# Six of eight expert weight splits done early, stored in DRAM, and loaded back as parts

## The chip, the cores and the metric

The kernel runs on one core of a Trainium2 chip. The metric is the device time of one execution in microseconds (us); smaller is better. The reader needs six names: PE is the matmul engine (TensorE), DVE, ACT and POOL are the vector, scalar and GpSimd engines, SP is the engine that issues most of the transfers, and a DMA queue is where an engine puts its transfers.

## The reference

A block of 16 batches of 128 tokens with 256 features goes through two residual layers. The first is cross-attention with 16 heads beside a gated feed-forward part. The second is a mixture of eight experts, two for each token, and a shared expert for all.

```
x = x + tanh(g_xattn) * (attention(LN(LN(x)), LN(ctx)) @ Wo + (silu(gate) * h) @ Wff2)
xf = LN(x)
shared = silu(xf @ sh_up_w + sh_up_b) @ sh_down_w + sh_down_b
scores = softmax(xf @ gate_w.T); the top 2 of 8, weights made to sum to 1 -> comb
h  = silu(einsum('nd,edh->neh', xf, up_w) + up_b)
ye = einsum('neh,ehd->ned', h, down_w) + down_b
x = x + tanh(g_ffn) * (einsum('ned,ne->nd', ye, comb) + shared)
```

## The kernel before

Every matrix product of f32 values is made of three passes of the PE: each operand is kept as a high part (the value rounded to the PE's format) and a low part (value minus high part), and `matmul3` adds low times high, high times high and high times low. So each weight has to be split once before it is used. The high part is an ACT copy, the low part a POOL subtraction.

The work stands in program order on each engine, written by hand, with semaphores between the engines. There are three stages.

*Attention* is eight passes (`iteration`, groups g = 0 to 7, two batches each) of eight steps s and a tail. In a step PE makes scores and one eighth of the feed-forward part, ACT makes the exponentials (L796) and copies of high parts (L788 for the feed-forward part), POOL scales the probabilities (L614) and makes a low part (L619), and DVE does the rest. In the first four steps POOL also issues one indirect transfer each (`send`, L606) that puts token rows of the pass before into `slot_rows` in DRAM, sorted by expert. SP loads one context tile in each pass and has little else to do from pass 1 to pass 6. In the last pass it writes filler rows to `slot_rows` (L509 to L514).

*The shared stage* follows: `shared_up` and `shared_down` for four blocks of 512 tokens, woven with the routing of the last group. The routing ends with `slot_numbers` on DVE (L1334), behind a wait until the rows of the group before have landed (L1471); it releases POOL's last four sends. `add_shared` (L1387) adds the shared expert's result on DVE.

*The tile loop* goes over 39 tiles of 128 rows. SP fetches a tile (L533, L535) into a ring of four, PE turns it (L1866), ACT and DVE split it (L913, L1504), PE multiplies by the expert's up weights, DVE adds the bias (L1500), ACT applies silu (L924), PE turns the result (L1872) and multiplies by the down weights, ACT scales it (L939), and POOL adds it to the output with an indirect transfer (L723). At tile 0 DVE also computes a table for POOL, `turn_table` (L1430 to L1441), between its work for tile 0 and that for tile 1.

The nine weight sets of this part (`shared` and experts 0 to 7, chunks 0 to 8) come through three staging buffers and one more: SP loads a chunk into a buffer, ACT writes the high part (`expert_hi`, L851, one copy of 128x1024), POOL the low part (`expert_lo`, L600, four subtractions of 128x256), and a chunk is loaded only when the one before it in its buffer is split (L473). Chunks 0 to 2 are loaded in pass 1. Chunk 0 and 1 are split in the last pass, chunk 2 right behind it, and 3 to 8 through the shared stage and into the tile loop, since their places in the big array `weights` hold attention's weights until then. The first four tiles wait for their expert alone, `ring_ready`, e + 2.

```
load_chunk(NCA + 8)                       # SP, L527: waits for the split of chunk 4
sp.wait_ge(dn_freed, USE_DOWN[0] + 2)     # L541, both halves of add_shared(0)
sp.dma_start(tiles_of(out, 0), xs[:, 0:TPS, :]).then_inc(written, 16)
sp.wait_ge(tables_done, 1)
sp.wait_ge(routed, 64 * (NG + 1))         # all sends landed
for t in range(4):
    load_tile(t, t)
```

## Time and profile before

| | |
|---|---|
| median of 3 runs | 549.81 us (549.61 to 549.9) |
| the profiled execution | 549.42 us, with a span of 547.6 us from its first to its last instruction |
| PE busy | 507.1 us, 93% of the span |
| DVE, ACT, POOL busy | 392.9, 329.6, 289.7 us |
| mean granted clock of PE | 0.975 of full speed |

The span is what the trace shows; the execution's own time is 1.8 us more. Times below count from the start of the span. In the pages' busy digits PE is at nine tenths in nearly all slices until about 425 us, then two slices are at 7 and 6; these are the end of the shared stage and the start of the tile loop. Attention lasts until about 404 us and the tile loop starts at about 436 us.

### The profile page before, as it was taken

The numbers are of one execution on the slowest core, as the hardware profiler recorded it, in microseconds if no ns is written. First come the engines' busy times: TensorE is split into PE (matmuls) and PEld (weight loads), VectorE is DVE, ScalarE is ACT, GpSimd is POOL, SyncE is SP. The second block draws the span as 40 slices with busy tenths as digits, with TensorE's granted clock in tenths as the row PEclk, the third lists the DMA queues.
The fourth block names the chain that finished last, engine by engine and source line by source line (L and its number), as shares of the span: only waits on it lengthen the run. The fifth ranks groups of instructions, "written<-read, shape, count | busy, mean of one in ns | idle before, by whom it ended". The sixth has DMA issues, their size and how long they took to land.

```text
span 547.6 us, 14295 instructions
## 1 busy us (share of the span) xinstructions
PE 507.1 (93%) x4081; PEld 489.9 (89%) x4082; DVE 392.9 (72%) x1179; ACT 329.6 (60%) x1074; POOL 289.7 (53%) x331
## 2 busy tenths in 40 slices
PE   7779999999999999999999999999999769998990
PEld 6779999999999999999999999999987759998980
DVE  7697777788787778878777887877687784554540
ACT  3667656656655565675656567565766626675750
POOL 4488535335443533544353354436666955488663
PEclk9999999999999999999999999999999958999996
DMA  5660400000100000010000000002967545588753
GB/s 169 201 219 6 134 13 32 21 2 20 40 0 8 24 28 0 21 37 3 4 27 29 0 20 20 1 12 71 345 183 243 168 136 88 97 131 128 115 79 38
DMA packets 41607, 39.88 MB, mean 73 GB/s; under 512 B 9939, under 2 KB 39588, under 8 KB 41444
## 3 DMA queue, kind: packets, MB, share of 16 engines
q1 hardware_dynamic: 33276, 27.63, 16.6%
q0 software_dynamic: 7968, 11.84, 11.7%
q8 instruction: 14, 0.23, 0.2%
q14 instruction: 19, 0.16, 0.1%
q10 hardware_dynamic: 330, 0.02, 0.0%
HBM read 20.55 MB, written 18.94 MB: 72 GB/s over the span
## 4 chain that ended last, share of the span: by engine, by line
PE 65%; DVE 16%; issue 6%; ACT 5%; DMA 3%; POOL 2%; SPq 1%; DVEq 0%; POOLq 0%; ACTq 0%
PE bank L1524 13%; PE bank L1525 12%; PE bank L1526 12%; PE bank L1605 4%; PE bank L1617 4%; PE bank L1710 4%; PE bank L1700 3%; PE bank L1621 2%; PE bank L1608 2%; DVE norm_probs L996 2%; ACT norm_probs L796 2%; PE bank L1539 2%; PE bank L1715 2%; DMA th<-slot_rows 2%; PE bank L1866 1%
## 5 line engine op out<-in xcount | busy, mean ns | idle before, releaser
L614 POOL TENSOR_TENSOR norm_probs<-norm_probs,rden 128x512 f32<-128x512 f32 x64 | 66.7, 1042 | 113.0 <-DVE rden L1183 112.3
L1524 PE MATMUL bank<-acts,weights 128*128 128x256 f32 x384 | 109.5, 285 | 4.6 <-POOL weights L585 2.2
L1525 PE MATMUL bank<-acts,weights 128*128 128x256 f32 x384 | 108.0, 281 | 0.0
L1526 PE MATMUL bank<-acts,weights 128*128 128x256 f32 x384 | 107.8, 281 | 0.0
L796 ACT ACTIVATE norm_probs<-bank,nmax 128x128 f32<-128x128 f32 x256 | 90.6, 368 | 24.3 <-DVE nmax L1139 24.3
L619 POOL TENSOR_TENSOR acts<-uf,acts 128x256 fp32r<-128x256 f32 x64 | 47.6, 744 | 69.0 <-ACT acts L788 69.0
L723 POOL DMA_INDIRECT out_x<-norm_probs,th x39 | 60.5, 1553 | 31.7 <-DMA out_x<-norm_probs,th 17.8
L1524 PEld LDWEIGHTS bank<-acts,weights 128*128 128x128 f32 x384 | 72.3, 188 | 5.5 <-issue 3.9
L1526 PEld LDWEIGHTS bank<-acts,weights 128*128 128x128 f32 x384 | 72.4, 189 | 0.0
L1525 PEld LDWEIGHTS bank<-acts,weights 128*128 128x128 f32 x384 | 72.3, 188 | 0.0
L788 ACT ACTIVATE acts<-uf 128x256 fp32r<-128x256 f32 x64 | 26.8, 419 | 69.9 <-DVE uf L1208 69.8
L1188 DVE TENSOR_TENSOR acts<-bank,acts 128x512 fp32r<-128x512 f32 x64 | 44.0, 687 | 22.3 <-ACT acts L778 20.2
L796 ACT ACTIVATION_READ_ACCUMULATOR norm_probs<-bank,nmax 128x1 f32 x256 | 52.7, 206 | 0.0
L1710 PE MATMUL bank<-weights,acts 128*128 128x256 f32 x256 | 46.0, 301 | 0.0
L1139 DVE TENSOR_REDUCE nmax<-bank 128x4 f32<-128x512 f32 x64 | 43.7, 682 | 2.2 <-PE bank L1526 1.7
L772 ACT ACTIVATE acts<-bank 128x256 fp32r<-128x256 f32 x64 | 24.4, 382 | 29.7 <-PE bank L1608 29.5
L606 POOL DMA_INDIRECT slot_rows<-spare,routing x36 | 36.4, 1010 | 10.5 <-issue 6.6
L1110 DVE TENSOR_TENSOR acts<-bank,acts 128x256 fp32r<-128x256 f32 x64 | 26.7, 417 | 20.5 <-ACT acts L772 20.2
L1700 PE MATMUL bank<-ident,norm_probs 128*128 128x128 f32 x256 | 38.7, 274 | 2.9 <-POOL norm_probs L614 2.8
L778 ACT ACTIVATE acts<-bank 128x512 fp32r<-128x512 f32 x64 | 38.9, 608 | 3.8 <-PE bank L1700 3.5
L1617 PE MATMUL bank<-weights,acts 128*128 128x256 f32 x256 | 40.4, 280 | 0.0
L1525 PE MATMUL bank<-kz_h,q_t 128*128 128x256 f32 x128 | 36.1, 282 | 0.0
(256 smaller groups left out, 1556.0 us busy)
## 6 DMA issues: line engine op xcount, KB each, us to landing
slot_rows<-tf SPq DMA_DIRECT2D x8, 680.0 KB, 6.7
spare<-slot_rows SPq DMA_DIRECT2D x39, 128.0 KB
ct<-in_ctx SPq DMA_DIRECT2D x8, 256.0 KB, 2.7
xs<-in_x SPq DMA_DIRECT2D x8, 256.0 KB, 5.1
out_x<-xs POOLq DMA_DIRECT2D x3, 512.0 KB, 4.1
stage<-in_L_ffn_up_w SPq DMA_DIRECT2D x5, 256.0 KB, 2.8
stage<-in_L_ffn_down_w SPq DMA_DIRECT2D x5, 256.0 KB, 3.2
xs<-in_L_xattn_Wff SPq DMA_DIRECT2D x4, 256.0 KB
```

What stands on the lines that cost most here:

```text
L614: pool.tensor_tensor(pr[:, s % 2], pr[:, s % 2], rden[:, s % 2, :].unsqueeze(2).broadcast_to((P, 4, P)), ALU.mult).then_inc(probs_ready, 1)
L619: pool.tensor_tensor(uT[1][:, s % 2, :], uf[:, :], uT[0][:, s % 2, :].bitcast(F32), ALU.subtract).then_inc(u_ready, 1)
L723: pool.indirect_dma_start(out_rows, bass.IndirectOffsetOnAxis(ap=meta[:, t, 0:1].bitcast(I32), axis=0), ys[:, at:at + D], None, compute_op ...
L796: done = act.activation(pr[:, s % 2, h, :], sc_ps[s % 2][:, h * P:(h + 1) * P], ACT.Exp, bias=nmax[:, s % 2, h:h + 1], accum_out=den[:, s ...
L1139: dve.tensor_reduce(nmax[:, s % 2, :], halves(sc_ps[s % 2], 4), AX.X, ALU.max, negate=True).then_inc(nmax_done, 1)
L1188: dve.tensor_tensor(pT[1][:, :], t_ps[:, :], pT[0][:, :].bitcast(F32), ALU.subtract).then_inc(pT_ready, 1)
L1524: pe.matmul(ps, wts[1], mov[0], start=first, stop=False, skip_group_check=True)
L1525: pe.matmul(ps, wts[0], mov[0], start=False, stop=False, skip_group_check=True)
L1526: return pe.matmul(ps, wts[0], mov[1], start=False, stop=last, skip_group_check=True)
L1617: pe.matmul(at, oT[0][:, m, :], w[:, 2 * (s // 2) + m, :], start=False, stop=False, skip_group_check=True)
L1700: done = pe.transpose(t_ps[:, h * P:(h + 1) * P], pr[:, (s - 1) % 2, h, :], ident[:, :])
L1710: pe.matmul(out_ps[:, b * D:(b + 1) * D], uT[0][:, (s - 1) % 2, b * P:(b + 1) * P], w[:, s - 1, :], start=s == 1 and b == 0 and n == 0, st ...
```

## The change

The splits of experts 2 to 7 move into passes 1 to 6, one expert a pass. SP loads the expert's weights as they are into the first staging buffer. In steps 2, 4, 5 and 7 of the pass ACT copies a quarter as high part into the second staging buffer and POOL subtracts, in place in the first. Then SP stores both parts into a new DRAM array, `parked`, in the order in which `weights` keeps them. Behind attention SP loads them straight to their places, one transfer of 1 MB for each expert: 2 to 4 behind the last feed-forward product of attention (`mix_filled`), 5 and 6 behind `ff2_done`, 7 behind `wo_done`. Chunks 1 and 2 (experts 0 and 1) are loaded between pass 6 and the filler rows. `ring_ready` now ends at 3, and PE's first tile waits for it and for all six loads (`weights_in`).

```diff
-NPOS = NE + 1
+NPOS = 3
+PARK_FROM = 2
+PARK_STEPS = (2, 4, 5, 7)
@@ SP
-            for c in range(3):
+            load_chunk(NCA)
+            split(sp, 8)
+            split(sp, 9)
+            for g in range(1, NG - 1):
+                if g > 1:
+                    sp.wait_ge(park_stored, 32 * (g - 1))
+                e = PARK_FROM + g - 1
+                for m, w in enumerate((up_w[e], down_w[e])):
+                    sp.dma_start(park_src[:, KT * m:KT * m + KT, :], w.rearrange("(k p) n -> p k n", p=P)
+                                 ).then_inc(stage_full[0], 16)
+                if g + 2 < NG:
+                    load_ctx(g + 2)
+                sp.wait_ge(park_lo, 4 * g)
+                for i, part in enumerate(park_parts):
+                    sp.dma_start(parked[e - PARK_FROM, :, i::2, :],
+                                 part.bitcast(F32).rearrange("p (m k) n -> p m (k n)", m=2)).then_inc(park_stored, 16)
+            sp.wait_ge(park_stored, 32 * (NG - 2))
+            for c in (1, 2):
                 load_chunk(NCA + c)
-            for g in range(3, NG):
-                load_ctx(g)
...
-            for c in range(3, 6):
-                load_chunk(NCA + c)
-            sp.wait_ge(pT_filled, NG * NU)
-            load_chunk(NCA + 6)
-            load_chunk(NCA + 7)
+            sp.wait_ge(mix_filled, mix_index(f"FF{NU - 1}", NG - 1, False, True) + 1)
+            for e in range(PARK_FROM, 5):
+                load_parked(e)
+            sp.wait_ge(ff2_done, NG * NU)
+            load_parked(5)
+            load_parked(6)
             sp.wait_ge(wo_done, NG * NU)
...
-            load_chunk(NCA + 8)
+            load_parked(7)
@@ POOL, in a pass
+                    if s in PARK_STEPS and not first and not last:
+
+                        k = PARK_STEPS.index(s)
+                        pool.wait_ge(park_hi, g * 4 + (k - 3))
+                        pool.tensor_tensor(park_parts[1][:, k], park_src[:, k], park_parts[0][:, k].bitcast(F32),
+                                           ALU.subtract).then_inc(park_lo, 1)
@@ POOL, behind the last pass
-            expert_lo(3)
...
-            expert_lo(4)
-            expert_lo(5)
-            store_tiles(1)
-            expert_lo(6)
-            store_tiles(2)
-            expert_lo(7)
-            store_tiles(3)
-            expert_lo(8)
+            for j in range(1, TPS):
+                store_tiles(j)
@@ ACT, in a pass, behind the tanh of step s
+                    if s in PARK_STEPS and not first and not last:
+
+                        k = PARK_STEPS.index(s)
+                        act.wait_ge(stage_full[0], g * 32 + stage_value(8))
+                        act.activation(park_parts[0][:, k], park_src[:, k], ACT.Copy).then_inc(park_hi, 1)
@@ ACT: expert_hi(3) to expert_hi(8) are gone
@@ PE, first tile
-                    if loop is None and t < 4:
-                        pe.wait_ge(ring_ready, e + 2)
-                    elif loop is None and t == 4:
-                        split(pe, NCA + NE)
+                    if loop is None and t == 0:
+                        pe.wait_ge(ring_ready, NPOS)
+                        pe.wait_ge(weights_in, 16 * (NE - PARK_FROM))
```

On SP, from the end of the filler rows to the first fetch of a tile, this is what stood there before. The `stage`, `xs` and `norm_probs` rows are the chunks to be split.

```order
L514 DMA slot_rows<-ct 128x16 x7
L475 DMA stage<-in_L_ffn_up_w 128x2x256
L475 DMA stage<-in_L_ffn_down_w 128x2x256
...
L475 DMA norm_probs<-in_L_ffn_up_w 128x2x256
L475 DMA norm_probs<-in_L_ffn_down_w 128x2x256
L475 DMA stage<-in_L_ffn_up_w 128x2x256
L475 DMA stage<-in_L_ffn_down_w 128x2x256
L522 DMA acts<-bias_copy 128x2048
L525 DMA acts<-bias_rows 1x2048 x2
...
L542 DMA out_x<-xs 128x4x256
L531 TENSOR_LOAD tf
```

And this stands there now, in the same place (line numbers are those of the changed kernel).

```order
L539 DMA slot_rows<-ct 128x16 x7
L543 DMA weights<-parked 128x2048 x5
L554 DMA acts<-bias_copy 128x2048
L557 DMA acts<-bias_rows 1x2048 x2
L543 DMA weights<-parked 128x2048
L574 DMA out_x<-xs 128x4x256
L563 TENSOR_LOAD tf
```

Twelve transfers of 256 KB that waited for splits have become six of 1 MB that wait for attention's last products alone, and the last of them no longer waits for POOL.

On POOL, from its last sends to its first scatter of the tile loop, this stood before (with the semaphores that each row waits for).

```order
L606 DMA slot_rows<-spare,routing 18816x272 [waits slots_done]
L606 DMA slot_rows<-spare,routing 18816x272 x3
L600 TENSOR_TENSOR weights<-stage,weights 128x256 [waits ring_hi_done]
L600 TENSOR_TENSOR weights<-stage,weights 128x256 x3
L600 TENSOR_TENSOR weights<-xs,weights 128x256 [waits ring_hi_done]
L600 TENSOR_TENSOR weights<-xs,weights 128x256 x3
L695 DMA out_x<-xs 128x4x256 [waits dn_freed]
L600 TENSOR_TENSOR weights<-norm_probs,weights 128x256 [waits ring_hi_done]
L600 TENSOR_TENSOR weights<-norm_probs,weights 128x256 x3
L695 DMA out_x<-xs 128x4x256 [waits dn_freed]
```

Now the same stretch is this.

```order
L638 DMA slot_rows<-spare,routing 18816x272 [waits slots_done]
L638 DMA slot_rows<-spare,routing 18816x272 x3
L732 DMA out_x<-xs 128x4x256 [waits dn_freed] x3
L754 DMA out_x<-norm_probs,th 2560x256 [waits y_added1,y_added0,y_added2,y_copied,y_added3,stored,turns_done,written]
```

The subtractions of chunks 4 to 8, 20 of them, no longer stand between the last send and the first scatter; chunk 3's four stood ahead of the last sends and are gone too.

In a pass of attention POOL has this now in steps 4 and 5. The rows on `stage` are new.

```order
L646 TENSOR_TENSOR norm_probs<-norm_probs,rden 128x512
L651 TENSOR_TENSOR acts<-uf,acts 128x256
L670 REGISTER_ALU
L671 TENSOR_TENSOR stage<-stage 128x256
L645 REGISTER_ALU
L646 TENSOR_TENSOR norm_probs<-norm_probs,rden 128x512
L651 TENSOR_TENSOR acts<-uf,acts 128x256
L662 REGISTER_ALU
L663 TENSOR_TENSOR spare<-spare,routing 128x2x8
L670 REGISTER_ALU
L671 TENSOR_TENSOR stage<-stage 128x256
```

So a part operation stands behind the low part of its step and ahead of the next scaling of probabilities. On PE and DVE the instructions are the same in number and order; only what they wait for differs, at PE's first tile and at the first row of `turn_table`.

## Rows read from the trace of the kernel before

**Rows 1.** The page, its first line.

```profile
span 547.6 us, 14295 instructions
```

**Rows 2.** Stretch, length, busy PE, PEld, DVE, ACT, POOL, PE clock, DMA share, GB/s.

```profile
180.00:232.00 52.00, 51.52 (x435) 50.85 (x434) 41.06 (x134) 32.66 (x120) 23.28 (x27) 1.00 0.06 19
...
440.00:450.00 10.00, 6.21 (x27) 5.22 (x27) 9.09 (x18) 2.08 (x6) 7.09 (x10) 0.50 0.53 160
```

**Rows 3.** The same columns in stretches of 2 us.

```profile
394.00:396.00 2.00, 2.00 (x19) 2.00 (x18) 1.35 (x10) 1.72 (x9) 2.00 (x4) 1.00 1.09 357
...
420.00:422.00 2.00, 2.00 (x15) 1.86 (x15) 1.72 (x12) 0.00 (x0) 0.00 (x0) 1.00 1.03 374
...
438.00:440.00 2.00, 0.95 (x3) 0.56 (x4) 1.88 (x4) 0.38 (x1) 0.00 (x0) 0.54 0.28 68
...
454.00:456.00 2.00, 2.00 (x14) 2.00 (x13) 1.01 (x3) 1.33 (x4) 1.35 (x1) 0.69 0.12 17
```

**Rows 4.** SP in order of time: start, us, engine, line, what.

```profile
402.86 0.43 SPq L475 DMA_DIRECT2D stage<-in_L_ffn_up_w  x1
...
430.88 0.40 SPq L475 DMA_DIRECT2D stage<-in_L_ffn_up_w  x1
...
431.84 0.46 SPq L542 DMA_DIRECT2D out_x<-xs  x1
433.35 0.36 SPq L533 DMA_DIRECT2D spare<-slot_rows  x1
```

**Rows 5.** PE in order of time, with idle time before and releaser.

```profile
436.99 0.41 PE L1866 MATMUL bank<-ident,spare 128*128 128x128 f32 x2 [1.27 <-DMA th<-slot_rows]
...
449.96 0.69 PE L1872 MATMUL bank<-ident,ct 128*128 128x128 f32 x2 [3.29 <-ACT ct L924]
```

**Rows 6.** DVE in order of time, the same columns.

```profile
421.69 0.17 DVE L1334 CAST routing<-routing 128x4 int32<-128x4 f32 x1
...
423.50 0.15 DVE L1403 SCALAR_TENSOR_TENSOR routing<-routing 1x8 f32<-1x8 f32 x1
423.69 0.16 DVE L1405 TENSOR_SCALAR ct<-routing 1x8 f32<-1x8 f32 x1
...
427.65 1.59 DVE L1387 SCALAR_TENSOR_TENSOR xs<-bank,gates,xs 128x512 f32<-128x512 f32 x2
...
437.86 0.42 DVE L1504 TENSOR_TENSOR kz_l<-bank,kz_h 128x256 fp32r<-128x256 f32 x1 [2.95 <-ACT kz_h L913]
...
443.08 0.71 DVE L1431 SCALAR_TENSOR_TENSOR xs<-xs,routing 1x8 f32<-1x8 f32 x1
...
447.28 0.45 DVE L1436 TENSOR_TENSOR xs<-tf,routing 1x294 f32<-1x294 f32 x1
...
449.04 0.42 DVE L1500 TENSOR_TENSOR uf<-bank,acts 128x256 f32<-128x256 f32 x1
```

**Rows 7.** POOL in order of time, behind attention.

```profile
414.14 1.22 POOL L606 DMA_INDIRECT slot_rows<-spare,routing  x1 [0.30 <-issue]
...
426.15 0.96 POOL L606 DMA_INDIRECT slot_rows<-spare,routing  x1 [0.31 <-issue]
...
444.44 2.78 POOL L600 TENSOR_TENSOR weights<-stage,weights 128x256 fp32r<-128x256 f32 x4
```

**Rows 8.** ACT, then POOL, then DVE in one pass.

```profile
194.25 0.42 ACT L788 ACTIVATE acts<-uf 128x256 fp32r<-128x256 f32 x1 [0.69 <-DVE uf L1208]
...
197.25 1.04 POOL L614 TENSOR_TENSOR norm_probs<-norm_probs,rden 128x512 f32<-128x512 f32 x1 [1.75 <-DVE rden L1183]
...
212.30 1.30 POOL L591 TENSOR_TENSOR acts<-tf,acts 128x512 fp32r<-128x512 f32 x1 [0.58 <-ACT acts L742]
...
195.66 0.73 DVE L996 TENSOR_SCALAR norm_probs<-ct,mean,ry 128x256 f32<-128x256 f32 x2
...
206.08 2.06 DVE L996 TENSOR_SCALAR norm_probs<-xs,mean,ry 128x256 f32 x2
```

**Rows 9.** Who waited for whom on PE, 100 to 355 us: total, times, longest.

```profile
PE bank L1621 <- DVE acts L1110: 2.5, 6, 0.5
```

More of the change, by code:

```diff
@@ L264, in program @@
         bias_rows = nc.dram_tensor("bias_rows", (2, 2 * NE + 1, D), F32).ap()
+        parked = nc.dram_tensor("parked", (NE - PARK_FROM, P, 4, KT * HID), F32).ap()
         bias_copy = nc.dram_tensor("bias_copy", (NE, HID), F32).ap()
@@ L283, in program @@
         ring_ready = sem("ring_ready")
+        park_hi = sem("park_hi")
+        park_lo = sem("park_lo")
+        park_stored = sem("park_stored")
+        weights_in = sem("weights_in")
         ident_done = sem("ident_done")
@@ L377, in buffer @@
                 return (stage[:, i, :] if i < 2 else spare[:, 0:1024] if i == 2 else slow_stage), i
-            i = (0, 1, 3, 0, 1, 3, 2, 0, 1)[n - NCA]
-            return (stage[:, i, :] if i < 2 else pr.rearrange("p s h n -> p (s h n)") if i == 2
-                    else slow_stage), i
+            i = (3, 0, 1)[n - NCA]
+            return (stage[:, i, :] if i < 2 else slow_stage), i
+        park_src = stage[:, 0, :].rearrange("p (k n) -> p k n", k=4)
+        park_parts = [stage[:, 1 - i, :].bitcast(F32R).rearrange("p (k n) -> p k n", k=4) for i in range(2)]
         def tile_loop(eng, step):
@@ L435, in stage_value @@
         def stage_value(n):
-            return 16 * sum(len(chunk_loads(m)) for m in range(n + 1) if buffer(m)[1] == buffer(n)[1])
+            parks = 32 * (NG - 2) if n >= NCA and buffer(n)[1] == 0 else 0
+            return 16 * sum(len(chunk_loads(m)) for m in range(n + 1) if buffer(m)[1] == buffer(n)[1]) + parks
         def landed(eng, n):
@@ L514, in _, with load_parked @@
                 sp.dma_start(pads[:, k, D:ROW], pad_pairs[k % 3].rearrange("p e k -> p (e k)")).then_inc(pads_stored, 16)
-            for c in range(3, 6):
-                load_chunk(NCA + c)
-            sp.wait_ge(pT_filled, NG * NU)
-            load_chunk(NCA + 6)
-            load_chunk(NCA + 7)
+            def load_parked(e):
+                sp.dma_start(experts[:, e * 2048:(e + 1) * 2048].bitcast(F32),
+                             parked[e - PARK_FROM].rearrange("p m n -> p (m n)")).then_inc(weights_in, 16)
+            sp.wait_ge(mix_filled, mix_index(f"FF{NU - 1}", NG - 1, False, True) + 1)
[4 more added lines that the diff above has]
+            load_parked(6)
             sp.wait_ge(wo_done, NG * NU)
@@ L564, in _ @@
             pool.dma_start(dbrow[0:1, :], sh_down_b.rearrange("(a n) -> a n", a=1)).then_inc(dbrow_in, 16)
-            pool.dma_start(dbrow[1:NPOS, :], down_b).then_inc(dbrow_in, 16)
+            pool.dma_start(dbrow[1:NE + 1, :], down_b).then_inc(dbrow_in, 16)
             pool.memset(ones.bitcast(F32), 1.0)
@@ L892, in _ @@
             hidden_hi(0)
-            expert_hi(3)
-            expert_hi(4)
             act.wait_ge(dn_filled, USE_X1T + 1)
@@ L931, in tile_step @@
                             act.wait_ge(y_added[n % 4], 16 * (n // 4))
-                        elif n == RING // 2 - 1:
-                            act.wait_ge(ring_ready, NPOS)
                     else:
@@ L1427, in turn_table @@
             def turn_table():
-                dve.wait_ge(ring_ready, NPOS - 3)
+                dve.wait_ge(ring_ready, NPOS)
                 link(dve.tensor_scalar(floor_0, ntiles, -float(P), 2.0 * P, ALU.mult, ALU.add))
```

6 lines of the change are left out of this document (removed).

## The prediction

> **What bounds the kernel now.** I read first the page and then the table of stretches. The profiled execution took 549.42 us, of which the span is 547.6 [rows 1]. In a stretch of attention PE is busy for 51.52 of 52 us, at full clock, while POOL is busy for 23.28 and ACT for 32.66 [rows 2]. From 100 to 355 us only one wait of PE has a length worth listing, 2.5 us in six pieces [rows 9]. So attention is bound by PE, and what the other engines do there is free as long as it comes in time. Between 440 and 450 us PE is busy for 6.21 of 10 us and its clock is at 0.50 of full speed, that is, at the lower of its two levels, 1.2 GHz [rows 2]. This stretch, where the shared stage gives way to the tile loop, is the only one that the change can shorten.
>
> The timelines of the engines say what PE waits for there. It ends the shared stage at 435.72 and waits 1.27 us for the first tile, whose transfers SP issued only at 433.35, behind the store of the first output block at 431.84, behind a chunk that had waited for POOL until 430.88 [rows 4, 5]. The store's own condition, both halves of `add_shared(0)`, had been met at 429.24 (427.65 + 1.59 [rows 6]). Then PE waits once more, 3.29 us before 449.96, for silu of tile 1 [rows 5]. ACT could not give that, since DVE added tile 1's bias only at 449.04 [rows 6]. Before it DVE worked on `turn_table`: six instructions on single rows of 7 or 8 elements, from 443.08 to 447.28, 4.20 us, or 0.70 us each. The same kind of instruction takes one step of 0.19 us at 423.50 [rows 6], when POOL is idle. POOL was subtracting meanwhile; its last four, of chunk 8, start at 444.44 and take 2.78 us [rows 7], and the fast pace of DVE returns as they end.
>
> **The change part by part.** *The first tile comes earlier.* SP no longer waits for POOL. It issues the store at 429.3, right behind 429.24, and the first tile's transfers 1.51 us later (433.35 - 431.84 [rows 4]), at 430.8 instead of 433.35. The tile took 3.6 us from there until PE used it (436.99 - 433.35), so it is there at 434.4, before PE has ended the shared stage. PE then turns it at 435.7 and not at 436.99: the idle 1.27 us are gone. (POOL at rest may also let DVE end its part of the shared stage some tenths earlier; I count nothing for it.) ACT's copy and DVE's subtraction of tile 0 (437.86 [rows 6]), `add_shared(2)`, `add_shared(3)` and the bias of tile 0 follow on each other and move with it: 1.27 us.
>
> *`turn_table` is not slowed.* Its six small instructions take six steps of 0.19 to 0.20 us instead of 4.20: 1.2, a gain of 3.0. Its longer ones came behind POOL's last subtraction already.
>
> The Trainium skill gives a reason for the pace (GPSIMD Engine Reference, Specifications): GpSimd's access to SBUF is shared with the vector engine, in contention with those of its instructions that have two inputs in SBUF or run in a two-port mode. The rows agree in so far as the slow steps end with POOL's work. The same rule speaks against the change in the passes, where POOL gets 24 more subtractions; that is the third rival.
>
> Both terms stand on one chain, DVE to the bias of tile 1, then ACT, then PE: 1.27 + 3.0 = 4.27 us. PE's restart moves from 449.96 to 445.7.
>
> *The clock.* In the trace it is at half from the stretch 438 to 440 (mean 0.54) until the stretch 454 to 456 (0.69, so it rose at 455.2) [rows 3]; PE had been without a gap since 449.96. At half speed these 5.2 us did the work of 2.6. After the change PE still idles in pieces: between 435.7 and 445.7 it has five tiles to turn (0.4 us each as at 436.99 [rows 5]), one silu result and three products of six matmuls, by my estimate 4 to 5 us of work in 10. I take it that the clock falls and comes back about as long after the restart as before: no term, with a rival at 2.6 us.
>
> *The passes.* ACT gets four copies of 128x256 a pass. An instruction of this size is 0.42 us, and the copy stands behind tanh, where ACT then idles for 0.69 us in the tightest step, step 4 [rows 8]. POOL gets four subtractions, 0.70 us each (2.78 for four [rows 7]). In step 4 it idles 1.75 us before the scaling [rows 8], and the part fits. In step 7 it idles 0.58 us before the low part of the next x [rows 8], so that one comes some 0.15 us later; it is wanted only behind the keys and values. SP's transfers are off the others' way: 0.5 MB in and 1 MB out in a pass whose DMA share is 0.06 [rows 2]. ACT waits for the weights in step 2. The store follows step 7 of the pass before; 1.57 MB at 357 GB/s [rows 3] is 4.4 us, and with twice the 3.6 us from issue to use of a tile 11.6. Step 2 comes about a third of a pass behind step 7, and eight passes end at about 404 us, so that is some 16 us. From both sides: nothing at the least, since PE has no wait to lose; at the most what stands under the third rival. I take nothing.
>
> *The loads behind attention.* From 402.86 [rows 4] SP issues six transfers of 1.05 MB and `up_bias` with 1.05 MB: 7.3 MB, twice as much as before. The trace moves 357 GB/s when saturated with stores, and 374 where `up_bias` alone, with rows of 8 KB as these have, goes through [rows 3]. At 357 this is 20.6 us: all is in at 423.5, 7 us before the first tile is fetched on the same queue and 13 before PE needs the weights. It costs nothing by itself. But POOL's four sends of the group before (the last at 414.14 [rows 7]) go through the same engines, and `slot_numbers` (421.69 [rows 6]) waits for them. They have 6.3 us from the end of issue (415.36) to need. A tile's transfer takes 3.6 us on a lightly used queue, which leaves 2.7 us for the crowd.
>
> *Removed from ACT*: six copies of 128x1024, where ACT waited anyway. No term.
>
> **The sum.** 549.42 - 4.27 = 545.15 for the profiled execution. The median of the runs is 0.39 us above it, so 545.5 for the median.
>
> **The rivals.** *The clock stays up* (18 in 100). If PE's pieces of work between 435.7 and 445.7 keep it up, the half-speed work behind the restart is saved too: 545.5 - 2.6 = 542.9. For it: 4 to 5 us of work in 10, against 0.95 in the two microseconds where it fell [rows 3]. Against it: a gap of 2 to 3 us before the restart stays. The Trainium skill says (TensorE: Matmul & The Clock Gate, the HAM clock gate) that a lack of activity throttles the clock to 1.2 GHz and that steady activity releases it; the trace shows both turns, and not where between the two patterns the boundary lies.
>
> *Only the table gains* (12 in 100). The tile's fetch stays as late, behind the stores of output blocks or the last loads on SP's queue: 3.0 us instead of 4.27, 546.8.
>
> *The sends starve* (16 in 100). If a saturated queue of 8 KB rows lets POOL's sends through only when it is empty, at 423.5, and they then take 0.5 us, `slot_numbers` comes at 424.2 and everything behind it 2.5 us later: 545.5 + 2.5 = 548.0. The Trainium skill (DMA: Bandwidth & Descriptors, Queues, rings and completion order) has the engines go round the queues packet by packet, which would let them through; no run here has shown it for rows of this size. This rival ends slower than before only if the loads run at under 7.3 MB / (425.5 - 402.9) = 323 GB/s, since then the delay is over 4.27 us.
>
> *The passes pay* (9 in 100), the one that ends on the other side. DVE's pair of scalings (L996) takes 0.73 us alone and 2.06 us when POOL works through it [rows 8]: 1.33 us more under about two of POOL's instructions, or 0.7 for each. In step 4 a part falls on such a pair (195.66). If PE had no slack behind two of the four parts of a pass, 2 x 0.74 x 6 = 8.9 us would be added: 554.4. It cancels the gain from 0.71 us a pass on (4.27 / 6) and is measurably slower from 0.90. Against it: PE waits for DVE 0.4 us a pass now [rows 9], and in the pair's step POOL and ACT both idle before their next pieces of work [rows 8].
>
> **How the numbers follow.** Forecast 45 in 100, 545.5, its own range 544.3 to 546.7. A measurement of this kernel can tell about 0.2%, 1.1 us. Faster by more: the forecast, the first two rivals and three quarters of the third, 45 + 18 + 12 + 12 = 87, less 3 for what I have not seen: 84. Within: 6. Slower: 10. The range that leaves 2 in 10 out goes from 542.0, below the first rival, to 548.4, above the third.
>
> **What would show it right or wrong.** In the new trace the stretch 100 to 355 has the same PE busy share, and attention still ends at about 404 us; SP's store comes at 429.3 and the first tile at 430.8; the six small rows of `turn_table` take 0.2 us each; PE's first L1872 (now in a new line) stands at about 445.7; the weights are in by 424. It is wrong if ACT's park copies wait for their transfer (then each pass is longer), if the DVE row of `slot_numbers` stands later than 421.7, or if the tile loop from the restart to the end is longer than its 97.7 us now (547.6 - 449.96), for instance because POOL's scatters, which run at the pace of the tiles, were the limit all along.

## The result and the profile after

Over four runs each the changed kernel takes 544.34 us (542.77 to 545.37) against 549.74 us (549.61 to 549.9) for the kernel before; the ratio is 0.9899, with a 95% interval of 0.9875 to 0.9923. Two more measurements, made with the experiments on other occasions, gave 0.9898 (0.9875 to 0.9922) and 0.9907 (0.9887 to 0.9927). The change makes the kernel 1% faster, some 5.4 us. The chips differ in level (one has the kernel before at 546.2 us), so below the times of kernels are compared within a group or as ratios. Of traces from different chips only the lengths of single stretches are compared.

The profiled execution of the changed kernel took 544.31 us, 5.11 less than the one of before, and the span is 5.1 us shorter [rows 1].

The windows, with the columns of [rows 2], show an unchanged pass and a fuller stretch at 440 to 450 us:

```profile
span 542.5 us, 14349 instructions
...
180.00:232.00 52.00, 51.52 (x435) 50.84 (x435) 41.93 (x130) 33.70 (x123) 26.26 (x30) 1.00 0.14 49
440.00:450.00 10.00, 8.14 (x54) 7.75 (x55) 7.13 (x23) 4.69 (x13) 2.33 (x3) 0.83 0.52 159
```

PE is busy for the same 51.52 us of 52, while POOL has 3.0 us and ACT 1.0 us more to do. In the later stretch PE is busy for 8.14 us in place of 6.21. The list of PE's waits from 100 to 355 us is the same to the tenth as in [rows 9]:

```profile
PE bank L1646 <- DVE acts L1135: 2.5, 6, 0.5
```

SP in order of time shows the first loads behind attention, the store of the first output block and the first fetches of tiles ([rows 4]):

```profile
402.89 2.56 SPq L543 DMA_DIRECT2D weights<-parked  x5
...
430.37 0.41 SPq L574 DMA_DIRECT2D out_x<-xs  x1
431.82 0.36 SPq L565 DMA_DIRECT2D spare<-slot_rows  x1
```

PE in order of time: the turns of tiles 0 and 1, and the restart ([rows 5]):

```profile
436.27 0.38 PE L1890 MATMUL bank<-ident,spare 128*128 128x128 f32 x2
437.47 0.44 PE L1890 MATMUL bank<-ident,spare 128*128 128x128 f32 x2 [0.82 <-DMA th<-slot_rows]
...
445.60 0.44 PE L1896 MATMUL bank<-ident,ct 128*128 128x128 f32 x2 [0.62 <-ACT ct L951]
```

DVE in order of time: `slot_numbers`, the first half of `add_shared(0)`, tile 0 with its bias, the short rows of `turn_table`, and the bias of tile 1 ([rows 6]):

```profile
422.81 0.17 DVE L1359 CAST routing<-routing 128x4 int32<-128x4 f32 x1
...
428.75 1.60 DVE L1412 SCALAR_TENSOR_TENSOR xs<-bank,gates,xs 128x512 f32<-128x512 f32 x2
...
437.11 0.42 DVE L1529 TENSOR_TENSOR kz_l<-bank,kz_h 128x256 fp32r<-128x256 f32 x1 [3.11 <-ACT kz_h L940]
...
441.22 0.42 DVE L1525 TENSOR_TENSOR u<-bank,acts 128x256 f32<-128x256 f32 x1 [0.34 <-issue]
...
442.35 0.15 DVE L1458 TENSOR_TENSOR xs<-xs 1x8 f32<-1x8 f32 x1
442.53 0.15 DVE L1459 TENSOR_TENSOR tf<-tf,xs 1x7 f32<-1x7 f32 x1
...
444.68 0.42 DVE L1525 TENSOR_TENSOR uf<-bank,acts 128x256 f32<-128x256 f32 x1
```

The rows of `turn_table` take 0.15 us each. In the kernel before the five behind the first took 0.71, 0.75, 1.38, 0.64 and 0.65 us; this is the longest:

```profile
444.50 1.38 DVE L1433 TENSOR_TENSOR xs<-xs 1x8 f32<-1x8 f32 x1
```

From the bias of tile 0 to that of tile 1 it is 3.46 us now; in the kernel before it was 6.89 us (442.15 to 449.04). PE goes from the shared stage into tile 0 without a wait.

Last the granted clock, the column in front of the last two, in windows of 2 us ([rows 3]):

```profile
402.00:404.00 2.00, 1.42 (x10) 1.42 (x11) 1.93 (x12) 1.10 (x3) 1.21 (x2) 0.83 0.27 30
404.00:406.00 2.00, 2.00 (x11) 2.00 (x11) 0.60 (x1) 0.00 (x0) 0.00 (x0) 0.50 0.82 303
...
440.00:442.00 2.00, 0.76 (x3) 0.76 (x4) 1.56 (x5) 0.52 (x2) 0.89 (x2) 0.72 0.68 236
442.00:444.00 2.00, 2.00 (x12) 2.00 (x11) 1.76 (x9) 0.70 (x3) 0.00 (x0) 0.50 1.00 332
444.00:446.00 2.00, 1.38 (x10) 1.03 (x9) 1.84 (x6) 0.85 (x3) 0.00 (x0) 0.93 0.45 104
```

Before, one fall lasted from 438 to 455 us. Now the clock is at half from 440.9 to 444.3 us (worked out from the means, as are all such times below), and before that from 403.3 to 406.8 us, at the end of attention, where the kernel before had none.

**Where the time went.** Each line is how much earlier (-) or later (+) a landmark stands in the new trace, and what was added since the line above. The last four are ACT's scaling of the results of a tile (L939 before, L964 after) and the end of the span.

```
landmark                                  before   after    diff   added here
PE ends the shared stage                  435.72   436.27  +0.55   clock fall at 403.3, less what DVE gained
PE turns tile 0                           436.99   436.27  -0.72   -1.27  no wait for the tile
DVE adds the bias of tile 0               442.15   441.22  -0.93   -0.21
DVE adds the bias of tile 1               449.04   444.68  -4.36   -3.43  turn_table
PE restarts with the silu of tile 1       449.96   445.60  -4.36    0
ACT scales tile 1                         455.63   449.16  -6.47   -2.11  full clock behind the restart
ACT scales tile 20                        495.97   491.50  -4.47   +2.00  in the tile loop
ACT scales tile 38                        534.49   529.30  -5.19   -0.72  in the tile loop
end of the span                           547.6    542.5   -5.1    +0.1
```

The first line is two things. Behind the fall of the clock `add_shared(0)` starts 1.10 us later (427.65 and 428.75 us). But DVE's next two operations on 128x512 took 2.25 us beside POOL's subtractions before (the first line below) and take 1.37 now; the second line is from e8_after_again, where they stand together. So `add_shared(1)` starts only 0.38 us later (431.33 and 431.71), and from `add_shared(0)` to PE's end of the stage it is 7.52 us now (428.75 to 436.27) and was 8.07 (427.65 to 435.72): 1.10 - 0.55 = 0.55.

```profile
429.16 2.25 DVE L1377 TENSOR_TENSOR q_t<-norm_probs,q_t 128x512 fp32r<-128x512 f32 x2
429.23 1.37 DVE L1402 TENSOR_TENSOR q_t<-norm_probs,q_t 128x512 fp32r<-128x512 f32 x2
```

### The profile page after: what moved, and what is told of

The parts are those of the page before. It is cut to its first block, busy times and chain, and to the rows that moved or that the text cites. A ratio compares the mean times of both kernels' runs of the same rounds, so it can differ in the third digit from the quotient of the medians.

```text
span 542.5 us, 14349 instructions
## 1 busy us (share of the span) xinstructions
PE 505.0 (93%) x4081; PEld 489.4 (90%) x4082; DVE 391.6 (72%) x1179; ACT 330.9 (61%) x1092; POOL 289.2 (53%) x331
## 4 chain that ended last, share of the span: by engine, by line
PE 66%; DVE 16%; issue 7%; ACT 5%; POOL 2%; DMA 2%; SPq 1%; DVEq 0%; POOLq 0%; ACTq 0%
PE bank L1549 13%; PE bank L1550 12%; PE bank L1551 12%; PE bank L1630 4%; PE bank L1735 4%; PE bank L1642 4%; PE bank L1725 3%; PE bank L1633 2%; PE bank L1646 2%; DVE norm_probs L1021 2%; ACT norm_probs L827 2%; PE bank L1564 2%; PE bank L1740 2%; DVE nmax L1164 1%; PE bank L1896 1%
```

## The experiments

Each group ran on one chip. In the first are e1, e2, e4 and e8, with the kernel before at 546.19 us; in the second e3, e5, e6 and e7, with it at 549.57 us; in the third e9 to e12, with it at 549.82 us. The second has no run of the changed kernel, so there the ratios to the kernel before are compared (0.9899, 0.9898 and 0.9907 for the changed kernel). What each was expected to do stands under it as it was written before the run.

**e8_after_again, e11_after_again: the changed kernel itself.**

> The changed kernel unchanged, once more, for how far its executions lie apart. Its first four lay between 542.8 and 545.4 us, and the profiled one showed a fall of the granted clock at 403.5 us for 3.4 us that the kernel before did not have there. Theory A (where the clock falls differs from execution to execution, and with it up to about 2 us): the median lies within 543.5 to 545 us, the spread is again over 1 us, and a profiled execution with another mean clock has its falls elsewhere. Rival B (the fall at 403.5 us belongs to the change): it stands there again in this profile, with the same length.

> The changed kernel once more, as the mark for the other kernels of this group on the same chip. It should lie at 0.990 of the kernel before, as in both measurements so far (0.9899 and 0.9898), within their intervals.

540.75 us (539.8 to 542.18), ratio 0.9898, and 544.67 us (543.19 to 546.09), ratio 0.9907. The first lies under the 543.5 to 545 us expected, on a chip where the kernel before is some 3.5 us faster too; the ratio is the same. The spread is 2.4 and 2.9 us. The falls of the clock in three profiled executions of one and the same kernel, each worked out from windows of 2 us, up to 455 us:

```
first profile                          403.3-406.8   440.9-444.3
e8_after_again    16.8-20.2, 30.4-33.8               440.0-443.4
e11_after_again   16.9-20.3, 30.6-34.0 429.9-433.4   443.6-450.4
```

So the fall at 403.3 us is not in every execution of the changed kernel. In e8_after_again, without it, it is 24.64 us from PE's wait at the end of attention to `add_shared(0)` (403.08 to 427.72), against 24.66 before (402.99 to 427.65), and SP's store and first fetch stand where the prediction had them:

```profile
429.34 0.41 SPq L574 DMA_DIRECT2D out_x<-xs  x1
430.79 0.36 SPq L565 DMA_DIRECT2D spare<-slot_rows  x1
```

In e11_after_again the same stretch is 25.35 us (403.27 to 428.62), with no fall of the clock in it. Here DVE waits for the sends, which it does in neither trace without the loads (before, e10_before_table_early):

```profile
422.68 0.17 DVE L1359 CAST routing<-routing 128x4 int32<-128x4 f32 x1 [0.82 <-DMA slot_rows<-spare,routing]
```

The last of these sends starts at 414.42 us, so it took about 8.3 us to land; the DVE row needs it 7.5 us after its start (421.69 - 414.14 before, 421.79 - 414.25 in e8_after_again). The same wait, of 0.3 to 0.6 us, stands in seven of the other nine traces with the loads. So the loads cost that path between nothing and 0.8 us.

All three profiles show a fall in the gap behind 440 us, and it lasts 3.4 us in two and 6.8 us in the third. The lengths of the stretches from PE's first turn of a tile on are these:

```
stretch                                  before   first   e8      e11
PE's turn of tile 0 to bias of tile 0      5.16    4.95    4.93    4.91
bias of tile 0 to bias of tile 1           6.89    3.46    3.45    3.44
bias of tile 1 to ACT's scaling of it      6.59    4.48    4.45    5.76
scaling of tile 1 to that of tile 20      40.34   42.34   40.56   40.35
scaling of tile 20 to that of tile 38     38.52   37.80   37.70   38.41
```

The shorter table (second line) comes back in all three. What the clock gives behind the restart is 2.1 us in two and 0.8 us in the third. The 2.00 us lost in the tile loop of the first profile are in neither of the others.

**e1_pool_busy: GpSimd subtracts again.**

```diff
-            for j in range(1, TPS):
-                store_tiles(j)
+            filled = [0]
+            def fill(n):
+                for _ in range(n):
+                    if filled[0]:
+                        pool.wait_ge(fill_done, filled[0])
+                    for k in range(4):
+                        done = pool.tensor_tensor(stage[:, 0, 256 * k:256 * k + 256], stage[:, 1, 256 * k:256 * k + 256],
+                                                  stage[:, 1, 256 * (3 - k):256 * (3 - k) + 256], ALU.subtract)
+                    done.then_inc(fill_done, 1)
+                    filled[0] += 1
+            fill(1)
+            store_tiles(1)
+            fill(2)
+            store_tiles(2)
+            fill(1)
+            store_tiles(3)
+            fill(1)
```

> The changed kernel with one addition: after its last sends GpSimd subtracts again, 20 dummy subtractions of 128x256 in groups of four, laid around the three stores of output tiles, into a buffer that nobody reads. They should keep GpSimd busy from about 428 to 447 us as in the kernel before, with nothing waiting for their result. Theory A (the small VectorE operations of `turn_table` are slowed while GpSimd subtracts): the small rows, 0.15 to 0.16 us in the changed kernel at 442.35 to 444.55, go back to about 0.70 us as in [rows 6], the table ends 3.0 to 3.4 us later and the time rises by 2.5 to 3.5 us, to 547 to 548 us. Rival B (the rows became short for a reason that has nothing to do with GpSimd, for example the order of the transfers around them): the rows stay under 0.2 us and the time stays within 1 us of 544.3 us.

543.83 us against 540.75 us for the changed kernel in the same group: 3.1 us slower, ratio 0.9952 (0.9936 to 0.9968). POOL and DVE in order of time:

```profile
440.87 2.80 POOL L743 TENSOR_TENSOR stage<-stage 128x256 f32<-128x256 f32 x4
443.63 0.77 POOL L733 DMA_DIRECT2D out_x<-xs  x1
444.42 3.25 POOL L743 TENSOR_TENSOR stage<-stage 128x256 f32<-128x256 f32 x4
```

```profile
441.72 0.61 DVE L1474 TENSOR_SCALAR xs<-routing 1x8 f32<-1x8 f32 x1
...
443.11 0.58 DVE L1477 TENSOR_TENSOR xs<-xs 1x8 f32<-1x8 f32 x1
443.73 0.15 DVE L1478 TENSOR_TENSOR tf<-tf,xs 1x7 f32<-1x7 f32 x1
...
444.55 0.95 DVE L1480 TENSOR_TENSOR xs<-tf,routing 1x294 f32<-1x294 f32 x1
```

Four of the six short rows, at 441.72, 442.36, 443.11 and 443.92 us, take 0.58 to 0.64 us. The other two, at 442.93 and 443.73, take 0.15, and one with 294 elements takes 0.95 instead of 0.45. Which row is long cannot be read off POOL's row beside it: 443.73 and 443.92 both start while POOL issues the store. The issue too can lengthen a row: in e4_table_early, where POOL subtracts nothing, the table's first row takes 0.48 us (434.96 to 435.44) under the issue of a store (434.65 to 435.48). A row that reduces one input is not longer, though it lies under the subtractions that start at 444.42:

```profile
446.43 0.45 DVE L1484 TENSOR_REDUCE xs<-xs 1x42 f32<-1x294 f32 x1
```

The table, from its first row to the bias of tile 1, takes 5.49 us (441.72 to 447.21); in e8_after_again it is 2.78 us (440.84 to 443.62). Theory A stands: nothing but GpSimd's work was added, nobody waits for its result, and more than half of the gain is gone. POOL's own stores come later by it (433.59, 440.04 and 443.63 us instead of 432.42, 438.30 and 440.15), but its first scatter still follows ACT's scaling of tile 0 by 1.5 us in both (450.36 to 451.83 and 446.00 to 447.46), so that is not the price. The clock is part of the price: it is at half from 440.3 to 454 us.

**e2_tile_late: the first tile later.**

```diff
-            sp.wait_ge(dn_freed, USE_DOWN[0] + 2)
+            sp.wait_ge(dn_freed, USE_DOWN[1] + 2)
```

> The changed kernel, with SyncE's store of the first output tiles, and so the fetch of the first gathered tile behind it, held until VectorE's second block of shared outputs is done, about 3 us later (store at about 433.5 instead of 430.4 us, first tile fetched at about 435 instead of 431.8). Theory A (the first tile's arrival is on the path: the 1.27 us of the prediction's sum): TensorE's first turn of a tile moves from 437.5 to about 440 us, the table of turns behind it as well, and the time rises by 2 to 3 us. Rival B (the table of turns on VectorE alone decides, and the first tile is hidden beside other work of VectorE): TensorE's restart at 445.9 us stays within 0.5 us and so does the time.

544.47 us against 540.75 us: 3.7 us slower, above the 2 to 3 expected, ratio 0.9956 (0.994 to 0.9973). PE waits for tile 0 again:

```profile
438.35 0.41 PE L1890 MATMUL bank<-ident,spare 128*128 128x128 f32 x2 [2.31 <-DMA th<-slot_rows]
```

DVE's first row of tile 0 stands at 439.22 us instead of 436.07. The tile was fetched at 434.25 us instead of 430.79, 3.5 us later: once PE waits for the tile, a late tile costs about its whole delay.

**e3_no_pass_split: passes without the arithmetic.**

```diff
@@ SP, in passes 1 to 6; ACT's and POOL's four operations each are gone
-                    sp.dma_start(park_src[:, KT * m:KT * m + KT, :], w.rearrange("(k p) n -> p k n", p=P)
-                                 ).then_inc(stage_full[0], 16)
+                    for i in range(2):
+                        sp.dma_start(parked[e - PARK_FROM, :, 2 * m + i, :].rearrange("p (k n) -> p k n", k=KT),
+                                     w.rearrange("(k p) n -> p k n", p=P)).then_inc(park_stored, 16)
```

> The changed kernel without the arithmetic that the passes pay: ScalarE's and GpSimd's eight operations a pass for the parts of experts 2 to 7 are gone, and SyncE copies the raw weights inside DRAM to both parts' places, so that the same 7.3 MB are loaded behind attention. The parts of these experts are therefore both the whole weights, and their outputs come out about twice too large; timing and routing depend on none of it. Theory A (the passes are bound by TensorE and pay nothing for the splitting, [rows 9]): attention ends where it ends in the changed kernel, within 0.5 us, and the time stays within 1 us of 540.7 us (this chip's changed kernel). Rival B (the passes pay for GpSimd's 3.0 us and ScalarE's 1.1 us more a pass): attention ends 2 to 6 us earlier and the time falls by as much.

544.65 us, ratio 0.9898 (0.9872 to 0.9924), the same as the changed kernel. The windows have PE at 51.52 us with POOL at 23.66:

```profile
180.00:232.00 52.00, 51.52 (x435) 50.86 (x434) 41.02 (x133) 32.71 (x123) 23.66 (x26) 1.00 0.12 39
```

PE's wait at the end of attention stands at 403.43 us, in the three profiles of the changed kernel at 402.58, 403.08 and 403.27, so attention does not end earlier. The 24 subtractions and 24 copies in the passes cost nothing that can be measured.

**e7_more_traffic and e9_one_mb: a longer queue.**

```diff
             load_parked(7)
+            sp.wait_ge(ring_ready, NPOS)
+            for i in range(3):        # range(1) in e9_one_mb
+                sp.dma_start(extra[i], experts[:, (i % 2) * 2048:(i % 2 + 1) * 2048].bitcast(F32)).then_inc(extra_stored, 16)
```

> The changed kernel with 3 MB more on SyncE's queue, directly behind the last parked weights: experts 0 and 1 copied out to a DRAM buffer that nobody reads, 8 KB a row like the loads. At the loads' 410 GB/s it lengthens the saturated stretch by about 7.5 us, from 424 to 431.5 us, over all of GpSimd's last sends (423.3 to 428.2 us) and up to the store of the first output tiles (430.4 us). Theory A (packets of the two queues alternate, so a send is only slowed, and there is over 1 us of slack): the first tile is fetched at most 1 us later and the time rises by 0 to 1 us. Rival B (the sends, or the store behind the extra transfer on its own queue, wait until the queue has run empty): the first tile is fetched 2 to 4 us later, TensorE's first turn with it, and the time rises by 2 to 4 us; then the prediction's slack of 6.3 us was real and had a threshold.

> As e7_more_traffic, but with 1 MB more behind the parked weights instead of 3. With 3 MB, SyncE waited 3.6 us for the sends before the first tile, and the time rose by about 3 us. 1 MB lengthens the saturated stretch by 2.5 us, to about 426.5 us, so that it covers two or three of the last four sends (423.3 to 428.2 us). Theory A (there is slack: the last sends need only be down by 431.8 us, when the store of the first output tiles has been issued): SyncE waits at most 0.3 us for the sends and the time stays within 0.8 us of the changed kernel. Rival B (every byte behind the weights costs in proportion, 1.2 us a MB): the time rises by about 1.1 us, with a wait of about 1 us for the sends.

With 3 MB the time is 547.31 us, ratio 0.9957 (0.9942 to 0.9972): more than half of the gain is gone. SP's waits, from 400 to 440 us, have an entry that the changed kernel does not have:

```profile
SPq L581 <- DMA slot_rows<-spare,routing: 3.6, 1, 3.6
```

```profile
431.68 0.39 SPq L579 DMA_DIRECT2D out_x<-xs  x1
436.63 0.36 SPq L570 DMA_DIRECT2D spare<-slot_rows  x1
```

The last send was issued at 428.55 us, and all had landed only at about 436.6 us; the engines' share had stayed at 0.98 or more from 418 to 436. In the changed kernel the last send is issued at 427.25 us, and by 431.82 SP had no wait for it. With 1 MB the time is 545.11 us, ratio 0.9922 (0.9904 to 0.9939), 0.4 us above the changed kernel of its group, and SP has no wait for the sends. So the last four sends have slack, and it ends somewhere between 1 and 3 MB. Whether the sends crept along between the other packets or stood until the queue was empty these two runs don't tell.

**e4_table_early: the table moved in the changed kernel; e10_before_table_early: the same move without the change.**

```diff
             window_table()
+            turn_table()
...
-                if isinstance(t, int) and t == 0:
-                    turn_table()
```

> The changed kernel, with `turn_table` moved on VectorE from the first tile's step (442.35 to 444.55 us) to a place right behind `window_table`, where VectorE stands idle from 433.6 to 437.1 us. Theory A (the table stands on the chain from the first tile to TensorE's restart): the restart at 445.9 us comes 2 to 2.5 us earlier and the time falls by 1.5 to 2.5 us, less what the clock takes, to about 542.3 us. Rival B (the clock takes it back: TensorE is just then at half clock, and an earlier restart works through more of it): under 0.7 us gained. Rival C (the table delays the first tile's own steps on VectorE): no gain or up to 1 us lost.

> The kernel before, without the change, with `turn_table` alone moved right behind `window_table`, where VectorE stands idle for 2.95 us until 437.9 us. GpSimd still subtracts there, so the small rows stay long (0.6 to 0.75 us, the table some 5.5 us). Theory A (the changed kernel's gain at the restart is that the table is short or away; the tile loop behind it takes part of any gain back): the time falls by 1.5 to 3.5 us, ratio 0.994 to 0.997, and the stretch at half clock gets shorter than the 17 us of the kernel before. Rival B (the table fits nowhere: it now delays the first tile's own steps by the 2.5 us that it exceeds the idle time, and these delay the restart): less than 1 us gained.

In the changed kernel the move gives nothing: 540.78 us against 540.75, where 1.5 to 2.5 us less were expected. The way to the restart did get shorter, with 2.01 us from the bias of tile 0 to that of tile 1 (442.39 to 444.40) in place of 3.45, but PE stood at half clock until 447.7 us. From the bias of tile 0 to ACT's scaling of tile 1 it is 7.85 us (442.39 to 450.24), in e8_after_again 7.90 (440.17 to 448.07): what the table gave, the slower work behind it took.

```profile
444.00:446.00 2.00, 2.00 (x11) 2.00 (x10) 1.27 (x3) 1.07 (x3) 0.00 (x0) 0.50 0.95 301
446.00:448.00 2.00, 2.00 (x12) 2.00 (x12) 1.27 (x3) 1.07 (x3) 0.00 (x0) 0.58 0.34 82
```

In the kernel before the same two lines give 546.85 us against 549.82, ratio 0.9962 (0.9946 to 0.9978): 3.0 us, where the whole change brings 5.2 in this group. The half clock lasts 10.1 us (440.0 to 450.1) in place of 17. DVE and then POOL in order of time; POOL's subtractions end at 438.04 us (435.27 + 2.77):

```profile
435.20 2.20 DVE L1430 TENSOR_SCALAR xs<-routing 1x8 f32<-1x8 f32 x1
437.43 0.64 DVE L1431 SCALAR_TENSOR_TENSOR xs<-xs,routing 1x8 f32<-1x8 f32 x1
438.00 0.15 DVE L1432 TENSOR_TENSOR xs<-xs,routing 1x8 f32<-1x8 f32 x1
```

```profile
435.27 2.77 POOL L600 TENSOR_TENSOR weights<-norm_probs,weights 128x256 fp32r<-128x256 f32 x4
```

One instruction on 8 elements takes 2.20 us here, and rows take 0.15 from about POOL's end on. The long rows have a pattern: 0.6 to 0.75 us is about one of POOL's subtractions (2.78 / 4 = 0.70), 1.38 about two, 2.20 about three. It looks as if a row waits for whole subtractions of its neighbour; no run was made to test it.

**e5_warm, e12_warm_again, e6_table_early_warm: idle products against the fall of the clock.**

```diff
+            def keep_warm(b, count):
+                for _ in range(count):
+                    pe.transpose(b[:, 0:P], ident[:, :], ident[:, :])
@@ at tiles 1 and 2, in front of the wait for silu; 8 more each at tile 0 and at the end of attention
+                    if isinstance(t, int) and t in (1, 2):
+                        keep_warm(b, WARM[t - 1])
                     pe.wait_ge(tile_silu_done, t)
```

> The changed kernel with idle transposes of the identity on TensorE in the gaps of the tile part: 8 ahead of the first tile's steps, 12 and 20 while it waits for VectorE at tiles 1 and 2, and 8 at the end of attention, all into banks that are overwritten afterwards. Theory A (the 3.4 to 4.5 us at half clock from 440.6 us on, which follow a stretch with TensorE busy 1.84 of 4 us, cost about 1.5 us of the time): the granted clock stays at 1.0 through 440 to 446 us and the time falls by 0.5 to 1.5 us. Rival B (TensorE waits for VectorE there at either clock, or the added transposes stand in the way of the real work): the time stays within 0.5 us or rises.

> The kernel of e5_warm again, beside the changed kernel on one chip. It gave 0.9886 of the kernel before, where the changed kernel gives 0.9899 and 0.9898. Theory A (keeping TensorE busy in the gaps is worth about 0.6 us): 0.988 to 0.989 again, and 0.4 to 1 us below the changed kernel of this group. Rival B (nothing): the medians within 0.4 us.

> Both at once: `turn_table` behind `window_table`, and TensorE's idle transposes in the gaps (8, 12 and 4 of them at tiles 0, 1, 2, and 8 at the end of attention). The table moved alone gave 540.8 us against 540.75 us of the changed kernel: TensorE's restart came 1.45 us earlier behind the first tile's bias, but stood at half clock until 447.2 us instead of 443.5. Theory A (the clock took the gain back): with the clock kept up the gain shows, and the time falls by 1.5 to 3 us below the changed kernel, to 538 to 539.5 us. Rival B (something else sets the start of the tile loop, such as the gathers of the tiles behind it): within 0.7 us of the changed kernel.

e5_warm gave 543.3 us, ratio 0.9886 (0.9862 to 0.991); again 543.77 us, ratio 0.9887 (0.9868 to 0.9906), which is 0.9 us under the changed kernel beside it, with overlapping intervals of the ratios. e6_table_early_warm gave 543.98 us, ratio 0.9895 (0.9871 to 0.992). None of them is clearly faster than the changed kernel, and the expectation for e6_table_early_warm, 538 to 539.5 us (for the first group's chip, 0.985 to 0.988 of before), was missed. The clock did what was wanted in two of the three profiles: in e12_warm_again and e6_table_early_warm it is at 1.00 through the gap; in e5_warm it fell at 438 us nevertheless, for 3.4 us. In e12_warm_again PE turns tile 1's silu 1.79 us behind its bias (444.11 to 445.90), in the changed kernel 0.92 (444.68 to 445.60): the twenty idle products stand in the way and cost at least part of what the clock gives. With the table away too, e6_table_early_warm is 0.84 us ahead of the changed kernel when ACT scales tile 0 (446.25 against 447.09 us) and 0.46 us behind at tile 8 (464.88 against 464.42). But one profile does not tell what a kernel does there. e5_warm and e12_warm_again are one kernel, and from the scaling of tile 8 to that of tile 20 it took 25.50 us in one and 27.35 in the other; e6_table_early_warm took 27.20. Why its time did not fall stays open.

## Why the prediction was right

The forecast, 545.5 us for the median, is 0.9922 of the kernel before; measured were 0.9899, 0.9898 and 0.9907. The likeliest case came in, with a sum that was 0.8 us short for the profiled execution (4.27 against 5.11). That it is so close is in part luck. The two terms of the sum measured 4.70. Around them stand pieces that it put at nothing: 2.11 us for the clock, 0.21 on the way to tile 0's bias and 0.55 for DVE's share in the shared stage to the one side, the clock's fall at 403.3 (1.10) and 1.28 in the tile loop to the other. The last two are in neither repeat.

*The first tile comes earlier (-1.27).* Right in the trace: the wait of 1.27 us is gone, and e2_tile_late shows that the tile is on the path. SP's store came at 430.37 and not at 429.3, and the fetch at 431.82, not 430.8, because DVE was 1.1 us later; both were issued directly behind DVE (428.75 + 1.60 = 430.35). In e8_after_again, without the clock's fall, they stand at 429.34 and 430.79. PE waited 0.82 us for tile 1, which the prediction did not look at.

*`turn_table` is not slowed (-3.0).* Right in place and cause, a little small: -3.43. The sum counted wrong here: the 4.20 us from 443.08 to 447.28 hold five instructions and not six; the sixth, at 442.82, took 0.22 us. The five take 0.83 now (442.08 to 442.91), where the sum had 1.2 for six. The cause is shown from two sides: e1_pool_busy brings long rows back with work that serves nothing, and in e10_before_table_early they end about as POOL ends. The rule that the prediction took from the Trainium skill (GPSIMD Engine Reference, Specifications) fits in part: the row that reduces one input stayed at 0.45 us beside POOL, and rows with two inputs in SBUF became longer. But the longest of all, 2.20 us, is a `TENSOR_SCALAR` with one input, which the rule covers only in a two-port mode, and no run shows in which mode it ran. The rows of the table are instructions on one partition; a row of 0.15 us mostly took 0.6 to 0.75, once 1.38 and once 2.20.

*The clock (no term).* This is the step that failed. The clock still falls, so the rival in which it stays up did not happen; but it did not come back as long after the restart as before. It was back at 444.3 us, before the restart at 445.60, and so the 5.2 us of work at half speed are gone: -2.11 from the restart to tile 1, where the rival had put 2.6. The prediction took the time from restart to recovery as fixed. The trace shows the recovery behind a run of PE's work: before, PE stood idle for 3.29 us in front of the restart [rows 5], now for 0.62 us. How much of it an execution gets varies: in e8_after_again it is 2.14 us, in e11_after_again, where the half clock lasted until 450.4 us, 0.83 (6.59 and 5.76 us from the bias of tile 1 to its scaling).

*DVE's end of the shared stage (no term).* The prediction said that POOL at rest might give some tenths here, and counted nothing. From `add_shared(0)` to PE's end of the stage it is 7.52 us in the first profile and in e8_after_again (427.72 to 435.24), against 8.07 before: 0.55 us. In e11_after_again the clock falls in this stretch, and it takes 9.06.

*The tile loop.* The prediction named a loop longer than 97.7 us as a sign of error. From the restart to the end it takes 96.9 us now, 94.7 in e8_after_again (444.54 to 539.2) and 96.5 in e11_after_again (446.96 to 543.5), so it is not longer. In the first profile 1.3 us of what the clock gave come back in it: from tile 8 to tile 20 it loses 1.8 us, with gaps of PE that have no releaser in the trace (2.1 us from 470 to 490 us, before 0.5), and behind tile 20 it gains 0.7. But this is that execution and not the change: from tile 1 to tile 20 the two repeats take 40.56 and 40.35 us, the kernel before 40.34. POOL's scatter-adds stand 1.85 us apart in both kernels for a long stretch (476.90 to 497.27 us for eleven steps before, 470.62 to 491.05 after). What sets the pace in the slow executions stays open; no experiment was made on it.

*The passes (nothing).* Right: the same PE busy time and the same waits with POOL's share up by 3.0 us a pass, and e3_no_pass_split takes the arithmetic away without a gain. The fourth rival is refuted.

*The loads (nothing).* Right for the loads, not quite for the sends beside them. The loads ran faster than the 357 GB/s of the estimate, at 404 to 434 GB/s in six of the seven windows from 408 to 422 us and at 357 in the other, and were in at about 424. In the first profile `slot_numbers` stands at 422.81 us and not at 421.7, which the prediction gave as a sign against it; this is the clock's fall at 403.3 us, since DVE has no wait in front of it, and in e8_after_again it stands at 421.79. In e11_after_again it stands at 422.68, and there it is the sends: 0.82 us of waiting. The prediction gave them 6.3 us from the end of the last issue and 2.7 of these to spare; this trace shows them landing 7.0 us behind it (415.64 to 422.68), so there was nothing to spare. The rival in which the sends starve, at 2.5 us, did not happen in this size, but a third of it did in one execution of three. e7_more_traffic shows that 3 MB more bring such a delay about for the last four sends.

## What to carry to other kernels

Work on one engine can lengthen another's instructions without any semaphore between them: compare the duration of the same small instruction in two places of one trace, and look at what the neighbour does in each. Before moving much work to get such a neighbour out of the way, try moving the few victims into idle time; here two lines gave 3.0 us where the whole change gave 5.2. And when a gap of PE gets shorter, count the clock as a term of its own, since the work behind the gap changes its speed with it. And profile one kernel more than once before a difference of 1 or 2 us in one stretch is put down to a change: here repeats took away two such readings, the clock's fall at the end of attention and the loss in the tile loop, and brought one, the wait for the sends.

## What was not expected of the hardware

- Executions of one program differ in where the granted clock falls (see the three profiles above), with 2.4 to 2.9 us between the fastest and slowest run.
- Transfers in rows of 8 KB moved 404 to 434 GB/s from DRAM into SBUF in most windows of 2 us, where stores under way had 357 [rows 3].
- Beside them the last of four indirect sends landed about 8.3 us after its start in one execution (414.42 to 422.68 us), and within 7.5 us in two others of the same kernel.
- Behind 3 MB of other traffic the last of four indirect sends landed about 8 us after its issue (428.55 to 436.6 us).
- Single-partition instructions of 8 elements took 0.15 us alone and up to 2.20 us beside GpSimd's subtractions of 128x256, which take 0.70 us each.
